# Attention scores with keys split once ahead and two heads a pass, and the order turns, scores, values on TensorE

## The chip, the core and the metric

The kernel runs on one core of one Trainium2 chip. The metric is the device time of one execution in microseconds (us), from the profiler's clock; the trace of one profiled execution shows what each engine did in it. An engine is TensorE (PE, with its weight loads shown apart as PEld), VectorE (DVE), ScalarE (ACT), GpSimd (POOL) or SyncE (SP, which here only issues DMAs).

## The reference

Two gated layers over 2048 tokens (16 blocks of 128) with 256 features: a convolution over context products, a mixture of experts with 8 routed experts (called f0), attention (called c), and a mixture with 32 routed experts (f1). The attention is where the change is:

```
x = x + tanh(g0[0]) * L0_xattn(ctx, ctx, layernorm(x), ...)     # context stage
x = x + tanh(g_ffn[0]) * L0_ffn(layernorm(x), ...)              # f0
x = x + tanh(g_xattn[1]) * L1_xattn(layernorm(x), ctx, ctx)     # attention, 16 heads of 16
x = x + tanh(g_ffn[1]) * L1_ffn(layernorm(x), ...)              # f1
# L1_xattn, with sequences of 128 tokens, so each block of 128 attends to itself:
scores = q @ k.T / 4 ; scores[k > q] = -inf ; p = softmax(scores) ; out = p @ v
```

Keys and values are both the context. The normed x and the keys are fp32, and the products of the scores are made in TensorE's reduced fp32 format (fp32r): each operand is split into a high part, rounded to it, and a low part, the rest.

## The kernel before

The four stages run one after the other, and each engine has its own written-out program; semaphores alone tie them. f0 and f1 walk over steps K: TensorE makes the hidden products of step K+1 (or K+4), then the output products of K. f0 has 64 steps of 18 or so passes of 512 columns.

The attention has 16 blocks b (128 tokens each) of 4 quads t (4 heads each), so 64 steps n = 4b + t. A step's work runs through all engines:

- scores (L1408 to L1419): into one of three PSUM banks go the causal mask (identity times a table, 512 columns, bf16), then `k_blocks_hi` and `k_blocks_lo`, each a pass of 512 columns over four heads. The stationary operand is `q_split_t`, whose 128 rows are 4 heads x 16 features for the high part and the same for the low part of the query. The moving operand is a block-diagonal array: the keys of head h stand in the rows of head h and the columns of head h, and zeros elsewhere. These blocks come from DRAM with their zeros, 256 KB a step (`load_keys`), ACT rounds them (`key_hi`, L1299) and POOL subtracts (`key_lo`, L1303), 60 times in the attention and 4 times at the end of f0.
- DVE takes each head's row maximum (`maxima`, L1598) and subtracts it into `y` (`shifted`, L1604).
- TensorE transposes `y`, four 128x128 (`turned`, L1426), ACT takes the exponential out of PSUM into `activated` (`probs`, L1567), and TensorE multiplies by the values (`values`, L1437): four products of 32 weight columns, each in its own strip of the array, which are 8 instructions in the trace since they are plain fp32.
- Once a block: the sum is copied out (`out_copy`, L1460, ACT), transposed (`out_rows`, L1446, at t = 2), and DVE divides by the sum of the probabilities, adds to X and takes moments (L1464, L1468, L1474, L1478). The queries of block b+3 are normed (L1310), rounded (L1317), subtracted (L1322, POOL); those of block b+2 are transposed (`query_turned`, L1330, four transposes at t = 3) and copied to `q_split_t` (`query_copy`, L1338).

TensorE's program in step n is: turned(n), scores(n+2), values(n), and what comes once a block. DVE's is maxima(n+1), shifted(n+1), and its once-a-block work. In steps 0 to 3 DVE also adds the last outputs of f0 to X (L241, L245); in steps 42 to 63 the first half of f1's inputs is prepared between the quads (transposes L332, router products L350, `x_lo` on DVE L342, rows L325 on ACT). In the trace, the turn of quad 0 starts at 402.73 us, that of quad 5 at 416.16, that of quad 42 at 486.95 and that of quad 63, the last, at 534.42.

```
                for n in range(NQ):
                    b, t = n // 4, n % 4
                    turned(pe, n)
                    if n + 2 < NQ:
                        scores(pe, n + 2)
                    ...
                    if n < NQ - 1:
                        values(pe, n)
```

## Time and profile before

| | |
|---|---|
| median of 3 runs | 937.21 us (936.82 to 937.28) |
| the profiled execution's own time | 935.47 us |
| its span, first to last instruction | 933.6 us |
| PE, PEld, DVE, ACT, POOL busy | 898.5, 719.5, 603.4, 551.0, 202.4 us |
| mean granted TensorE clock | 0.99 of full speed |
| attention, steps 5 to 41 | 70.79 us for 37 steps |
| attention, steps 42 to 62 | 47.47 us for 21 steps |

How to read it: a PE row's duration runs from a pass's start until its results are out, and passes are pipelined, so the distance from one start to the next says more than the duration. PE can look busy all the time while the starts stand further apart than the work needs. The PE record of L1418 begins early, at the end of its weights' request; its stream starts when that of L1414 is over.

### The profile page before, as it was taken

How to read it: one execution, taken by the hardware profiler on the slowest of the kernel's cores; microseconds unless marked ns; L12 is line 12 of the kernel's file. 1: busy time of each engine (PE TensorE's matmuls, PEld its weight loads, DVE VectorE, ACT ScalarE, POOL GpSimd, SP SyncE). 2: the span in 40 equal slices, each digit the busy share in tenths (PEclk: the TensorE clock that was granted, in tenths of full speed). 3: DMA queues.
4: the chain of work that ended last, by engine and by line, in shares of the span. 5: the costliest groups of instructions: out<-in, count | busy, mean ns of one | idle time of the engine just before them, and what ended most of it. 6: DMA issues, size and time to landing. Idle time of an engine off the chain costs nothing.

```text
span 933.6 us, 13901 instructions
## 1 busy us (share of the span) xinstructions
PE 898.5 (96%) x4704; PEld 719.5 (77%) x4704; DVE 603.4 (65%) x1390; ACT 551.0 (59%) x955; POOL 202.4 (22%) x172
## 2 busy tenths in 40 slices
PE   5899899999999999989999989999999999999998
PEld 5798788777788888856666667777788888888886
DVE  6678664465564566588888776566855466656654
ACT  3222343434444335468889677677777877777774
POOL 5899320000000012147777530000000000000000
PEclk9799999999999999999999999999999999999999
DMA  9101020333311351215554315434444244444443
GB/s 301 68 2 68 7 62 1 109 108 91 96 51 39 114 173 66 59 57 170 170 170 167 117 30 169 131 125 142 137 142 139 93 136 140 154 147 136 152 128 104
DMA packets 57957, 104.36 MB, mean 112 GB/s; under 512 B 7296, under 2 KB 13824, under 8 KB 57504
## 3 DMA queue, kind: packets, MB, share of 16 engines
q1 hardware_dynamic: 57168, 103.34, 34.5%
q8 instruction: 38, 0.62, 0.3%
q14 instruction: 31, 0.25, 0.1%
q10 hardware_dynamic: 720, 0.14, 0.1%
HBM read 101.03 MB, written 2.42 MB: 111 GB/s over the span
## 4 chain that ended last, share of the span: by engine, by line
PE 88%; DVE 5%; ACT 2%; POOL 1%; issue 1%; DMA 1%; SPq 1%; DVEq 0%; ACTq 0%; POOLq 0%
PE bank L646 37%; PE bank L682 28%; PE bank L1426 3%; PE bank L1437 2%; PE bank L1111 2%; PE bank L1113 2%; PE bank L1114 2%; PE bank L1126 2%; PE bank L1419 1%; PE bank L1418 1%; PE bank L350 1%; PE bank L1414 1%; PE bank L332 1%; DMA toeplitz<-in_kpad 1%; PE bank L1446 1%
## 5 line engine op out<-in xcount | busy, mean ns | idle before, releaser
L444 ACT ACTIVATE y_hi<-y 128x512 fp32r<-128x512 f32 x200 | 124.1, 621 | 82.2 <-DVE y L525 81.6
L539 DVE TENSOR_TENSOR y<-y,gate_rows 128x512 f32<-128x512 f32 x124 | 85.7, 691 | 120.6 <-ACT y L433 118.2
L682 PE MATMUL bank<-y_hi,w_hi 128*128 128x512 f32 x400 | 157.0, 393 | 1.5 <-DVE y_lo L308 1.0
L682 PE MATMUL bank<-y_lo,w_hi 128*128 128x512 f32 x400 | 156.5, 391 | 0.0
L682 PE MATMUL bank<-y_hi,w_lo 128*128 128x512 f32 x400 | 155.9, 390 | 0.0
L308 DVE TENSOR_TENSOR y_lo<-y,y_hi 128x512 fp32r<-128x512 f32 x196 | 134.3, 686 | 30.0 <-ACT y_hi L444 29.6
L427 ACT ACTIVATE activated<-bank 128x512 f32<-128x512 f32 x136 | 81.3, 597 | 80.9 <-PE bank L646 76.2
L646 PE MATMUL bank<-x_hi_first,w_hi 128*128 128x512 f32 x264 | 106.2, 402 | 0.7 <-DVE w_lo L303 0.7
L646 PE MATMUL bank<-x_hi_first,w_lo 128*128 128x512 f32 x264 | 104.2, 395 | 0.0
L646 PE MATMUL bank<-x_lo_first,w_hi 128*128 128x512 f32 x264 | 104.1, 394 | 0.0
L646 PE MATMUL bank<-x_hi_last,w_hi 128*128 128x512 f32 x264 | 103.9, 394 | 0.0
L646 PE MATMUL bank<-x_hi_last,w_lo 128*128 128x512 f32 x264 | 102.9, 390 | 0.0
L646 PE MATMUL bank<-x_lo_last,w_hi 128*128 128x512 f32 x264 | 102.7, 389 | 0.0
L1303 POOL TENSOR_TENSOR k_blocks_lo<-k_blocks_sb,k_blocks_hi 128x512 fp32r<-128x512 f32 x64 | 82.0, 1282 | 59.5 <-ACT k_blocks_hi L1299 59.0
L682 PEld LDWEIGHTS bank<-y_hi,w_hi 128*128 128x128 f32 x400 | 75.0, 188 | 20.4 <-DVE y_lo L308 2.9
L433 ACT ACTIVATE y<-activated 128x512 f32<-128x512 f32 x136 | 86.0, 632 | 4.3
L682 PEld LDWEIGHTS bank<-y_hi,w_lo 128*128 128x128 f32 x400 | 75.1, 188 | 16.3
L682 PEld LDWEIGHTS bank<-y_lo,w_hi 128*128 128x128 f32 x400 | 75.1, 188 | 16.2
L425 ACT ACTIVATE activated<-bank 128x512 f32<-128x512 f32 x64 | 38.3, 598 | 78.8 <-PE bank L646 78.8
L303 DVE TENSOR_TENSOR w_lo<-w_raw,w_hi 128x512 fp32r<-128x512 f32 (+1 forms) x96 | 75.1, 782 | 10.8 <-ACT w_hi L299 4.9
L299 ACT ACTIVATE w_hi<-w_raw 128x512 fp32r<-128x512 f32 (+1 forms) x100 | 69.7, 697 | 12.5 <-PE bank L682 12.5
L646 PEld LDWEIGHTS bank<-x_hi_first,w_hi 128*128 128x128 f32 x264 | 49.5, 188 | 12.5 <-DVE w_lo L303 1.0
(153 smaller groups left out, 1474.2 us busy)
## 6 DMA issues: line engine op xcount, KB each, us to landing
gate_rows<-gates SPq DMA_DIRECT2D x156, 256.0 KB, 3.7
w_raw<-in_wu SPq DMA_DIRECT2D x68, 256.0 KB, 2.6
k_blocks_sb<-in_k_blk SPq DMA_DIRECT2D x64, 256.0 KB, 4.2
w_raw<-in_wu SPq DMA_DIRECT2D x32, 384.0 KB, 3.1
v_slot<-in_v_rows SPq DMA_DIRECT2D x16, 256.0 KB, 2.6
ctx_windows<-in_ctx_win SPq DMA_DIRECT2D x3, 1024.0 KB, 11.8
toeplitz<-in_kpad SPq DMA_DIRECT2D x4, 512.0 KB, 8.7
X<-in_x SPq DMA_DIRECT2D x4, 512.0 KB, 9.2
```

Source lines behind the costliest of these rows:

```text
L299: act.activation(mem.whi[:, Nu % S, 0:WC], mem.wraw[:, Nu % S, 0:WC], ACT.Copy).then_inc(s_wh, 1)
L303: eng.tensor_tensor(mem.wlo[:, Nu % S, 0:WC], mem.wraw[:, Nu % S, 0:WC], mem.whi[:, Nu % S, 0:WC].bitcast(F32), ALU.subtract).then_inc(s_w ...
L308: eng.tensor_tensor(mem.ylo[:, K % S, :], mem.y[:, K % S, :], mem.yhi[:, K % S, :].bitcast(F32), ALU.subtract).then_inc(s_yl, 1)
L425: act.activation(mem.r[:, K % S, :], bk(2 * K % 3), ACT.Silu).then_inc(s_ac, 1)
L427: act.activation(mem.r[:, K % S, :], bk(K % 3), ACT.Relu).then_inc(s_ac, 1)
L433: act.activation(mem.y[:, K % S, :], mem.r[:, K % S, :], ACT.Square).then_inc(s_sq, 1)
L444: act.activation(mem.yhi[:, K % S, :], mem.y[:, K % S, :], ACT.Copy).then_inc(s_yh, 1)
L539: dve.tensor_tensor(mem.y[:, K % S, :], mem.y[:, K % S, :], gate, ALU.mult).then_inc(s_yd, 1)
L646: last = pe.matmul(o, w_[:, Nu % S, wc], x_[p][:, c, xs], start=(m == 0), stop=(m == 5))
L682: last = pe.matmul(acc(s)[:, c, :], w_[:, Nu % S, wc], y_[:, K % S, :], start=(n == 0 and m == 0), stop=(n == U - 1 and m == 2), skip_grou ...
L1303: pool.tensor_tensor(K2[:, n % KR, :], KM[:, n % KLR, :], K1[:, n % KR, :].bitcast(F32), ALU.subtract).then_inc(s_k2, 1)
L1426: last = pe.transpose(turn_bank(n)[:, g * P:(g + 1) * P], Ds[:, n % DR, g, :], ident[:])
```

## The change

Keys. The host no longer builds block-diagonal arrays. The keys come in as rows of 128 x 256 per block (`k_rows`). During f0, eight times, two blocks are loaded, ACT rounds them (`split_hi`), POOL subtracts (`split_lo`), and SP stores high and low parts to a DRAM tensor `k_parts` (`store_parts`, four DMAs each). The tiles that hold them are `v_slot` and `xn_split`, which the attention uses later. POOL then sets the eight `k_blocks` slots to zero once (a memset of 128 x 4096). In the attention, `load_keys` writes only the nonzero blocks, 64 partitions x 1 KB, in two DMAs a step (128 KB a step), eight slots deep; `key_hi` and `key_lo` are gone.

Scores. The 128 contraction rows are now 2 heads x (2 query parts) x (2 key parts) x 16 features, so one pass holds all four partial products of two heads and makes 256 columns. A step has two such passes (a = 0, 1), each with its own weights, in place of two passes of 512 columns over the same weights. The low-by-low product is now in.

Queries. There is twice as much of them: `query_hi` and `query_lo` write 512 columns in place of 256, with each part copied twice; `query_turned` and `query_copy` run twice a block, at t = 3 for a = 0 and at t = 0 of the next block for a = 1 (on ACT at t = 0 and t = 1). The transposes are fp32r with a rounded identity `ident_r`, in place of plain fp32.

Order. TensorE's step n is turned(n), scores(n+2), values(n-1). On ACT, `out_copy` of the block before stands behind `probs` of t = 0.

```diff
-                    if not final and K == NK - 16:
-                        attention_loads(sp)
+                    if not final:
+                        if K in (16, 18):
+                            load_raw(sp, (K - 16) // 2)
+                        if 21 <= K < 45 and K % 3 == 0:
+                            i = (K - 21) // 3
+                            store_parts(sp, i)
+                            if i + 2 < NB // 2:
+                                load_raw(sp, i + 2)
+                        if K == NK - 16:
+                            attention_loads(sp)
...
+                    for i in range(NB // 2):
+                        split_lo(pool, i)
+                    blocks_zeroed(pool)
...
+                        if 19 <= K < 43 and K % 3 == 1:
+                            split_hi(act, (K - 19) // 3)
...
-        KLR, KR, SR, DR, PR = 6, 4, 3, 3, 3
+        KR, SR, DR, PR = 8, 3, 3, 3
-        KM = sb("k_blocks_sb", [P, KLR, 4 * P])
-        K1 = sb("k_blocks_hi", [P, KR, 4 * P], F32R)
-        K2 = sb("k_blocks_lo", [P, KR, 4 * P], F32R)
+        K1 = sb("k_blocks", [P, KR, 4 * P], F32R)
-        xs = sb("xn_split", [P, 2, 4, 2, 64], F32R)
-        Q1 = sb("q_split_t", [P, 2, 4, P], F32R)
+        xs = sb("xn_split", [P, 2, 4, 2, P], F32R)
+        Q1 = sb("q_split_t", [P, 2, 2, 4, P], F32R)
...
+        def split_places(i):
+            parts = xs[:, i % 2].rearrange("p t a f -> p (t a f)")
+            return V[:, i % 2].rearrange("p h d -> p (h d)"), parts[:, 0:2 * D], parts[:, 2 * D:4 * D]
+
+        def load_raw(sp, i):
+            if i >= 2:
+                sp.wait_ge(s_k2, i - 1)
+            sp.dma_start(split_places(i)[0].rearrange("p (b f) -> p b f", b=2),
+                         k_rows[2 * i:2 * i + 2].rearrange("b p f -> p b f")).then_inc(s_kr[i % 2], 16)
+
+        def split_hi(act, i):
+            act.wait_ge(s_kr[i % 2], 16 * (i // 2 + 1))
+            if i >= 2:
+                act.wait_ge(s_ks[i % 2], 64 * (i // 2))
+            raw, high, _ = split_places(i)
+            act.activation(high, raw, ACT.Copy).then_inc(s_k1, 1)
...
+        def split_lo(pool, i):
+            pool.wait_ge(s_k1, i + 1)
+            raw, high, low = split_places(i)
+            pool.tensor_tensor(low, raw, high.bitcast(F32), ALU.subtract).then_inc(s_k2, 1)
+
+        def store_parts(sp, i):
+            sp.wait_ge(s_k1, i + 1)
+            sp.wait_ge(s_k2, i + 1)
+            for part, rows in enumerate(split_places(i)[1:]):
+                for j in range(2):
+                    place = k_parts[2 * i + j].rearrange("(g s d) f -> g s d f", s=2, d=HD1)[:, part]
+                    sp.dma_start(place, rows[:, j * D:(j + 1) * D].bitcast(F32)).then_inc(s_ks[i % 2], 16)
+
+        def blocks_zeroed(pool):
+            pool.memset(K1[:].rearrange("p n f -> p (n f)").bitcast(F32), 0.0).then_inc(s_kz, 1)
+
         def load_keys(sp, n):
-            if n >= KLR:
-                sp.wait_ge(s_k2, n - KLR + 1)
-            sp.dma_start(KM[:, n % KLR, :], k_blk[n]).then_inc(s_kl[n % KLR], 16)
+            if n >= KR:
+                sp.wait_ge(s_s, n - KR + 1)
+            for hh in range(2):
+                first = k_parts.offset + (2 * P * (n // 4) + 64 * (n % 4) + 32 * hh) * D
+                place = bass.AP(k_parts.tensor, first, [[0, 2], [D, 2 * HD1], [1, D]])
+                sp.dma_start(K1[64 * hh:64 * hh + 64, n % KR, hh * D:hh * D + D].bitcast(F32), place).then_inc(s_kl[n % KR], 16)
...
-        def key_hi(act, n):
-            act.wait_ge(s_kl[n % KLR], LOADED + 16 * (n // KLR + 1))
-            if n >= KR:
-                act.wait_ge(s_s, n - KR + 1)
-            act.activation(K1[:, n % KR, :], KM[:, n % KLR, :], ACT.Copy).then_inc(s_k1, 1)
-
-        def key_lo(pool, n):
-            pool.wait_ge(s_k1, n + 1)
-            pool.tensor_tensor(K2[:, n % KR, :], KM[:, n % KLR, :], K1[:, n % KR, :].bitcast(F32),
-                               ALU.subtract).then_inc(s_k2, 1)
...
+        def copies_of(view):
+
+            return view.rearrange("p (g f) -> p g f", f=HD1).unsqueeze(2).broadcast_to((P, NH1, 2, HD1))
+
+        def part_rows(b, part):
+            return xs[:, b % 2].rearrange("p t a (h s d f) -> p (t a h) s d f", h=2, d=2, s=2)[:, :, part]
+
         def query_hi(act, b):
             act.wait_ge(s_n, b + 1)
             if b >= 2:
-                act.wait_ge(s_xt, b - 1)
-            act.activation(xs[:, b % 2, :, 0, :], xc[:, b % 2, :].rearrange("p (q f) -> p q f", q=4),
-                           ACT.Copy).then_inc(s_hi, 1)
+                act.wait_ge(s_xt, 2 * (b - 1))
+            else:
+                act.wait_ge(s_ks[b], 64 * (NB // 4))
+            act.activation(part_rows(b, 0), copies_of(xc[:, b % 2, :]), ACT.Copy).then_inc(s_hi, 1)
 
         def query_lo(pool, b):
             pool.wait_ge(s_hi, b + 1)
-            pool.tensor_tensor(xs[:, b % 2, :, 1, :], xc[:, b % 2, :].rearrange("p (q f) -> p q f", q=4),
-                               xs[:, b % 2, :, 0, :].bitcast(F32), ALU.subtract).then_inc(s_lo, 1)
-
-        def query_turned(pe, b):
+            pool.tensor_tensor(part_rows(b, 1), copies_of(xc[:, b % 2, :]), part_rows(b, 0).bitcast(F32),
+                               ALU.subtract).then_inc(s_lo, 1)
+
+        def query_turned(pe, b, a):
+            if b + a == 0:
+                pe.wait_ge(s_ir, 1)
             pe.wait_ge(s_lo, b + 1)
-            if b > 0:
-                pe.wait_ge(s_qt, b)
+            if b + a > 0:
+                pe.wait_ge(s_qt, 2 * b + a)
             for t in range(4):
-                last = pe.transpose(x_bank[:, t * P:(t + 1) * P],
-                                    xs[:, b % 2, t].rearrange("p s f -> p (s f)").bitcast(F32), ident[:])
+                last = pe.transpose(x_bank[:, t * P:(t + 1) * P].bitcast(F32R), xs[:, b % 2, t, a, :], ident_r[:])
             last.then_inc(s_xt, 1)
 
-        def query_copy(act, b):
-            act.wait_ge(s_xt, b + 1)
+        def query_copy(act, b, a):
+            act.wait_ge(s_xt, 2 * b + a + 1)
             if b >= 2:
                 act.wait_ge(s_s, 4 * (b - 1))
-            act.activation(Q1[:, b % 2].rearrange("p t q -> p (t q)"), x_bank, ACT.Copy, scale=SCALE1).then_inc(s_qt, 1)
+            act.activation(Q1[:, b % 2, a].rearrange("p t q -> p (t q)"), x_bank, ACT.Copy, scale=SCALE1).then_inc(s_qt, 1)
...
         def attention_loads(sp):
-            for n in range(KLR):
+            for i in range(2):
+                sp.wait_ge(s_ks[i], 64 * (NB // 4))
+            sp.wait_ge(s_kz, 1)
+            for n in range(KR):
                 load_keys(sp, n)
...
-            if left in (12, 11, 4):
-                query_normed(act, {12: 0, 11: 1, 4: 2}[left])
-            if left in (11, 10, 3):
-                query_hi(act, {11: 0, 10: 1, 3: 2}[left])
-            if left in (9, 8, 7, 6):
-                key_hi(act, 9 - left)
-            if left in (6, 3):
-                query_copy(act, {6: 0, 3: 1}[left])
+            if left == 16:
+                act.activation(ident_r[:], ident[:], ACT.Copy).then_inc(s_ir, 1)
+            if left in (15, 13, 4):
+                query_normed(act, {15: 0, 13: 1, 4: 2}[left])
+            if left in (14, 12, 3):
+                query_hi(act, {14: 0, 12: 1, 3: 2}[left])
+            if left in (10, 7, 4, 1):
+                query_copy(act, (10 - left) // 6, (10 - left) // 3 % 2)
 
         def attention_ahead_pe(pe, left):
 
-            if left in (8, 5):
-                query_turned(pe, {8: 0, 5: 1}[left])
+            if left in (12, 9, 6, 3):
+                query_turned(pe, (12 - left) // 6, (12 - left) // 3 % 2)
...
-                pe.wait_ge(s_k2, n + 1)
+                pe.wait_ge(s_kl[n % KR], LOADED + 32 * (n // KR + 1))
                 if t == 0:
-                    pe.wait_ge(s_qt, b + 1)
-                pe.matmul(s_bank(n), Q1[:, b % 2, t, :], K1[:, n % KR, :], start=False, stop=False)
-                pe.matmul(s_bank(n), Q1[:, b % 2, t, :], K2[:, n % KR, :], start=False, stop=True).then_inc(s_s, 1)
+                    pe.wait_ge(s_qt, 2 * b + 2)
+                blocks = K1[:, n % KR, :].rearrange("p (h a k) -> p h a k", h=2, a=2)
+                for a in range(2):
+                    last = pe.matmul(s_bank(n)[:, a * 2 * P:(a + 1) * 2 * P], Q1[:, b % 2, a, t, :], blocks[:, :, a, :],
+                                     start=False, stop=(a == 1))
+                last.then_inc(s_s, 1)
...
-                for n in range(KLR, NQ):
+                for n in range(KR, NQ):
                     load_keys(sp, n)
...
                     turned(pe, n)
                     if n + 2 < NQ:
                         scores(pe, n + 2)
-                    if n == 0:
+                    if n == 1:
                         pe.wait_ge(f0.s_xa, 5)
-                    if n < NQ - 1:
-                        values(pe, n)
+                    if n > 0:
+                        values(pe, n - 1)
...
                     if t == 3 and b + 2 < NB:
-                        query_turned(pe, b + 2)
+                        query_turned(pe, b + 2, 0)
+                    if t == 0 and b > 0 and b + 1 < NB:
+                        query_turned(pe, b + 1, 1)
...
+                    if t < 2 and b > 0 and b + 1 < NB:
+                        query_copy(act, b + 1, t)
+                    probs(n)
                     if t == 0 and b > 0:
                         out_copy(act, b - 1)
-                    probs(n)
-                    if t == 0 and b > 0 and b + 1 < NB:
-                        query_copy(act, b + 1)
...
-                    if n + KR < NQ:
-                        key_hi(act, n + KR)
```

TensorE's program in the middle of the attention, before (L1437 values, L1426 turned, L1414 the mask, L1418 and L1419 scores, L1446 out_rows at t = 2):

```order
L1437 MATMUL bank3<-activated,v_slot 32x128 x4
L1426 MATMUL bank2<-ident,y 128x128 x4
L1414 MATMUL bank0<-causal,identb 128x512
L1418 MATMUL bank0<-k_blocks_hi,q_split_t 128x512
L1419 MATMUL bank0<-k_blocks_lo,q_split_t 128x512
L1437 MATMUL bank3<-activated,v_slot 32x128 x4
L1446 MATMUL bank3<-ident,o_t 128x128 x4
L1426 MATMUL bank2<-ident,y 128x128 x4
```

and the same place of the changed kernel (L1492 values, L1481 turned, L1466 the mask, L1472 scores, L1501 out_rows, L1382 query_turned):

```order
L1492 MATMUL bank3<-activated,v_slot 32x128 x4
L1501 MATMUL bank3<-ident,o_t 128x128 x4
L1481 MATMUL bank2<-ident,y 128x128 x4
L1466 MATMUL bank1<-causal,identb 128x512
L1472 MATMUL bank1<-k_blocks,q_split_t 128x256 x2
L1492 MATMUL bank3<-activated,v_slot 32x128 x4
L1382 MATMUL bank1<-ident_r,xn_split 128x128 x4
L1481 MATMUL bank2<-ident,y 128x128 x4
L1466 MATMUL bank0<-causal,identb 128x512
L1472 MATMUL bank0<-k_blocks,q_split_t 128x256 x2
```

The two passes of 512 columns have become two of 256. The values rows stand in the same place between scores and turns, but they are now those of the quad before.

ScalarE's program over one block before (L1460 out_copy, L1567 probs, L1338 query_copy, L1299 key_hi, L1310 query_normed, L1317 query_hi):

```order
L1460 ACTIVATE o_t<-bank 128x512
L1567 ACTIVATE activated<-bank 128x512
L1338 ACTIVATE q_split_t<-bank 128x512
L1299 ACTIVATE k_blocks_hi<-k_blocks_sb 128x512
L1567 ACTIVATE activated<-bank 128x512
L1299 ACTIVATE k_blocks_hi<-k_blocks_sb 128x512
L1567 ACTIVATE activated<-bank 128x512
L1299 ACTIVATE k_blocks_hi<-k_blocks_sb 128x512
L1310 ACTIVATE xn_c<-X,neg_mean_scaled,rstd 128x256
L1567 ACTIVATE activated<-bank 128x512
L1299 ACTIVATE k_blocks_hi<-k_blocks_sb 128x512
L1317 ACTIVATE xn_split<-xn_c 128x4x64
```

and after (L1389 query_copy, L1622 probs, L1515 out_copy, L1352 query_normed, L1368 query_hi):

```order
L1389 ACTIVATE q_split_t<-bank 128x512
L1622 ACTIVATE activated<-bank 128x512
L1515 ACTIVATE o_t<-bank 128x512
L1389 ACTIVATE q_split_t<-bank 128x512
L1622 ACTIVATE activated<-bank 128x512 x2
L1352 ACTIVATE xn_c<-X,neg_mean_scaled,rstd 128x256
L1622 ACTIVATE activated<-bank 128x512
L1368 ACTIVATE xn_split<-xn_c 128x16x32
```

The four roundings of keys a block are gone and one more copy of queries has come, ahead of the exponentials of t = 0 and t = 1.

## Rows read from the trace of the kernel before

**Rows 1.** Stretches: length, busy (x) of PE, PEld, DVE, ACT, POOL, clock, DMA, GB/s.
```profile
140.00:340.00 200.00, 199.41 (x895) 160.42 (x895) 109.68 (x208) 83.39 (x133) 2.64 (x2) 1.00 0.27 86
402.73:416.16 13.43, 10.60 (x90) 6.45 (x88) 13.09 (x33) 7.35 (x14) 6.01 (x6) 1.00 0.18 53
416.16:486.95 70.79, 70.47 (x628) 45.69 (x628) 61.95 (x123) 58.17 (x110) 54.72 (x48) 1.00 0.51 170
486.95:534.42 47.47, 45.24 (x393) 28.88 (x389) 39.42 (x69) 37.38 (x72) 31.96 (x28) 1.00 0.43 144
```

**Rows 2.** Waits in 416.16 to 486.95: us in total, times, longest.
```profile
PEld bank L1437 <- ACT activated L1567: 16.4, 37, 0.4
```

**Rows 3.** One step in order of time: start us, us, engine, line, xcount [idle before].
```profile
448.22 0.16 PEld L1437 LDWEIGHTS bank<-activated,v_slot 128*32 128x32 f32 x8 [0.44 <-ACT activated L1567]
448.25 0.69 DVE L1598 TENSOR_REDUCE max<-bank 128x4 f32<-128x512 f32 x1 [0.29 <-PE bank L1419]
448.57 0.42 PEld L1426 LDWEIGHTS bank<-ident,y 128*128 128x128 f32 x4 [0.20 <-issue]
448.96 0.10 PEld L1414 LDWEIGHTS bank<-causal,identb 128*128 128x128 bf16 x1
448.97 0.69 DVE L1604 TENSOR_TENSOR y<-bank,max 128x512 f32<-128x512 f32 x1
449.07 0.38 PE L1414 MATMUL bank<-causal,identb 128*128 128x512 bf16 x1
...
449.27 0.60 ACT L1567 ACTIVATE activated<-bank 128x512 f32<-128x512 f32 x1 [0.49 <-PE bank L1426]
449.29 0.19 PEld L1419 LDWEIGHTS bank<-k_blocks_lo,q_split_t 128*128 128x128 f32 x1
449.51 0.39 PE L1419 MATMUL bank<-k_blocks_lo,q_split_t 128*128 128x512 f32 x1
...
449.92 0.16 PEld L1437 LDWEIGHTS bank<-activated,v_slot 128*32 128x32 f32 x8 [0.44 <-ACT activated L1567]
```

**Rows 4.** Context stage, PE in order of time: passes of plain fp32.
```profile
70.09 1.57 PE L1111 MATMUL bank<-pair_products,toeplitz 128*128 128x208 f32 x8
71.50 1.04 PE L1126 MATMUL bank<-ident,weighted 128*128 128x128 f32 x8
```

**Rows 5.** End of f0 in order of time: fp32r weights loaded with nothing ahead.
```profile
372.51 0.19 PEld L646 LDWEIGHTS bank<-x_hi_last,w_hi 128*128 128x128 f32 x1
372.54 0.48 PE L646 MATMUL bank<-x_hi_last,w_hi 128*128 128x512 f32 x1
```

**Rows 6.** Weight loads at a change from whole array to 32 rows.
```profile
515.54 0.42 PEld L1446 LDWEIGHTS bank<-ident,o_t 128*128 128x128 f32 x4 [0.20 <-issue]
516.12 0.32 PEld L363 LDWEIGHTS bank<-ident,logits_t 32*128 32x128 f32 x4 [0.17 <-issue]
```

**Rows 7.** DVE in order of time, over its once-a-block work.
```profile
450.97 0.26 DVE L1464 RECIPROCAL rden<-bank 128x16 f32<-128x16 f32 x1 [0.34 <-PE bank L1446]
451.14 0.63 DVE L1604 TENSOR_TENSOR y<-bank,max 128x512 f32<-128x512 f32 x1
451.69 0.41 DVE L1468 TENSOR_TENSOR o_norm<-bank,rden 128x256 f32<-128x256 f32 x1
452.13 0.48 DVE L1474 SCALAR_TENSOR_TENSOR X<-o_norm,tg,X 128x256 f32<-128x256 f32 x1
452.54 0.68 DVE L1598 TENSOR_REDUCE max<-bank 128x4 f32<-128x512 f32 x1
453.14 0.42 DVE L1478 BATCH_NORM_STATS2 stats<-X 128x6 f32<-128x256 f32 x1
```

**Rows 8.** The same DVE line later, 508 to 511.
```profile
508.95 1.43 DVE L1474 SCALAR_TENSOR_TENSOR X<-o_norm,tg,X 128x256 f32<-128x256 f32 x1
```

**Rows 9.** POOL in the same stretch.
```profile
508.81 1.28 POOL L1303 TENSOR_TENSOR k_blocks_lo<-k_blocks_sb,k_blocks_hi 128x512 fp32r<-128x512 f32 x1 [0.37 <-ACT k_blocks_hi L1299]
```

**Rows 10.** SP's queue in order of time.
```profile
445.23 1.86 SPq L1288 DMA_DIRECT2D k_blocks_sb<-in_k_blk  x4
```

29 lines of the change are left out of this document (14 added, 15 removed).

## Prediction

> **What bounds the kernel now.** I read the stretches first [rows 1]. In f0 TensorE is busy 199.4 of 200 us; in steps 5 to 41 it is busy 70.47 of 70.79 us, DVE 61.95, ACT 58.17, POOL 54.72; steps 0 to 4 belong to DVE (13.09 of 13.43). A busy PE is not yet a fast PE, so next the waits: the weight loads of values waited for the exponential in all 37 steps, 16.4 us in total [rows 2]. Then one step by its start times [rows 3]. From the load of values at 448.22 to that of 449.92 it takes 1.70 us, in these pieces:
> - values to turned: 448.57 - 448.22 = 0.35.
> - turned to the stream of the mask: 449.07 - 448.57 = 0.50.
> - mask to the first keys pass: 449.29 - 449.07 = 0.22. The load of the second keys pass starts as the first stream does, so 449.29 marks it.
> - first to second keys pass: 449.51 - 449.29 = 0.22 to 0.23.
> - second keys pass to the load of values: 449.92 - 449.51 = 0.41. The exponential ends at 449.27 + 0.60 = 449.87, and the load starts 0.05 later.
>
> So the step is a loop: turn, exponential, values, turn, with the scores beside the exponential. Nothing that only shortens the scores would help; the new order is what opens this. Check of the whole stretch: 37 steps x 1.70 = 62.9 us; 70.79 - 62.9 = 7.9 us are 18 batches of four transposes (nine of `out_rows`, nine of `query_turned`), 0.44 each.
>
> **TensorE's step after the change.** The first two pieces and the mask stay: 0.35 + 0.50 + 0.22 = 1.07.
>
> First to second keys pass. A 256-column fp32r pass is not in the trace. The 512-column one has a pitch of 0.226, so half its columns make 0.11 to 0.12, if the next weights are in by then. What an fp32r load needs: with nothing ahead of it, it starts at 372.51 and its pass ends at 372.54 + 0.48 = 373.02 [rows 5]; a pass's record that is not held up is 0.39 [rows 3], so the stream began at 372.63, 0.11 to 0.12 after the load. The other end is the recorded load, 0.19 [rows 3]. Between them lies the plain fp32 pass of 208 columns: eight in 71.50 - 70.09 = 1.41, 0.176 each [rows 4]. I take 0.12, since load and stream both fit in it.
>
> The Trainium skill ("TensorE: Matmul & The Clock Gate", section "LDWEIGHTS (loading the stationary operand)") has a load take its column count over 1.2, which is 107 ns for 128 columns. By that the pass would be paced as I take it, and by the recorded 0.19 the sum below would lose 0.07 a step. What no row here shows: the same page in "What overlaps and what doesn't" lets a load overlap a running pass only in another row group, which would expose every load of the two shorter passes; the row of the second keys pass, whose load starts at 449.29 under a running stream, disagrees. It would give 58 x 2 x 0.11 = 12.8 more, 939, close to rival D below, and has no chance of its own.
>
> Second keys pass to values. Its stream is 0.12, and the array changes from whole to strips. The one other change of that kind is from `out_rows` to 32-row transposes [rows 6]: the next load comes 516.12 - 515.54 = 0.58 after the four transposes' first load, against 448.96 - 448.57 = 0.39 without such a change [rows 3]. The last transpose streams from about 0.39 to 0.50, so the change waits some 0.09 beyond the stream. The piece is 0.12 + 0.09 = 0.21. Upper bound: 0.41 - 0.11 = 0.30, if the wait seen today is the array's and not the exponential's (both would fit the 0.05). The exponential of quad n-1 ends 0.65 + 0.65 = 1.3 after that quad's turn, which is before turned(n), so values(n-1) waits for nobody.
>
> The step becomes 1.07 + 0.12 + 0.21 = 1.40, a gain of 0.30.
>
> **Batches.** `query_turned` runs twice a block. Today's fp32 transposes take (1.04 - 0.27)/7 = 0.11 each [rows 4]; an fp32r transpose is not in the trace. Half a 256-column pass would be 0.06, the recorded load 0.19. I keep 0.11, that is 0.44 a batch, the nearest row. A block is then 4 x 1.40 + 3 x 0.44 = 6.92 against 4 x 1.70 + 2 x 0.44 = 7.68.
>
> **Does DVE keep up?** Its work is unchanged. From max to shift 0.72 [rows 3], from shift to the next operation about 0.60, so a plain step needs 1.32. At t = 3 [rows 7]: max 0.60, reciprocal 0.17, then 0.55, 0.44, 0.41, together 2.17. At t = 0: 0.60, moments 0.42 by their duration, 0.60, together 1.62. A block needs 2 x 1.32 + 2.17 + 1.62 = 6.43, under 6.92. In latency: scores(n+2) are ready about 0.50 + 0.22 + 0.12 + 0.28 + 0.04 = 1.16 after turned(n) starts, max and shift end 1.41 later, so turned(n+2) could start at 2.6; two steps take at least 2.8, and those with batches 3.2. The reserve is thin but positive.
>
> **The other engines.** An ACT operation on 128 x 512 takes 0.6 [rows 3]; ACT loses four of them a block, the roundings, and gains one copy and half of one in `query_hi`, so about 1.5 us a block less. Its copies ahead of the exponential at t = 0 and 1 push it by at most 0.6, and its reader is now a step later. POOL loses 1.28 a step [rows 9]. SP issues eight key DMAs and one of values a block; four take 1.86 [rows 10], so 8 x 0.47 + 0.33 = 4.1 of 6.9 us. The loads run eight steps ahead, 8 x 1.7 = 14 us; today's six are 6 x 1.9 = 11. In f0: eight roundings on ACT and eight subtractions on POOL (idle there) of 0.6 and 1.3 us, in an f0 step of 18 passes x 0.23 = 4.1. SP stands in `store_parts` until they are done, with `gate_rows` and weights queued behind; it runs four steps ahead of their users and loses about two and a half. The memset and 16 first key loads (7.5 us of issue) come in a stage where the same four steps of 4.1 cover them.
>
> What could uncover f0: DVE's x update took 1.43 when a POOL subtraction had started 0.14 before it, and 0.48 otherwise [rows 7 to 9]. By the Trainium skill ("SBUF — State Buffer", section "SBUF: two separate sides"), a VectorE operation with two SBUF inputs and a GpSimd operation that reads SBUF lock each other out; the rows agree. It speaks against the eight subtractions in f0 and for the 60 that go. DVE is idle 45% of f0 [rows 1], 1.9 us of each 4.1, more than one subtraction of 1.28. I cost it at nothing; with the cover gone it is at most 8 x 1.28 = 10.2 us.
>
> **Sum**, against the profiled execution's own 935.5:
> - steps 0 to 4: nothing, DVE paces them.
> - steps 5 to 41: 37 x 0.30 = -11.1; nine more batches, +4.0: -7.1.
> - steps 42 to 62: 21 x 0.30 = -6.3; four more batches, +1.8; TensorE stood still there for 47.47 - 45.24 = 2.2 us [rows 1], while ACT and POOL were full of keys; of that I count -1.4. Against it the preparation of f1 goes through DVE's `x_lo` between quads, which a shorter step uncovers: +1.5. Together -4.4.
> - f0: two more batches of query transposes, +0.9.
>
> The sum is -10.6, so 924.9; the median stands 1.7 above the profiled time, so **926.6**.
>
> **Rivals.**
> - A, as above, TensorE paces at 1.40 to 1.45: 923 to 929. Chance 0.48.
> - B, the change to strips costs what it seems to today: second pass to values 0.30. 58 steps x 0.09 = +5.2: 932. For it: no step shows values without the exponential just done. Against: rows 6. Chance 0.15.
> - C, the fp32r transpose goes at 0.06: 4 x 0.05 in each of 30 query batches (18 in steps 5 to 41, 8 after, 4 in f0) = -6.0; a block is then 6.5, next to DVE's 6.43: 920.6. Chance 0.15.
> - D, the other side: the recorded 0.19 of an fp32r load sets the pace of every short pass. 58 steps x 0.07 = +4.1, 30 query batches x 4 x 0.08 = +9.6: 940, slower. For it: the change makes 128 short passes and 128 short transposes, and the one short non-transposing pass goes at 0.176, not at its recorded load's 0.19 but not below either. Against: the load in rows 5. The gain of 10.6 is used up at 10.6/(58 + 120) = 0.06 above 0.11, so from 0.17 on. Chance 0.10.
> - E, gains are given back in waits: DVE late after its t = 3 work, f1's preparation, or the eight subtractions in f0; half the gain: 930 to 935. Chance 0.12.
>
> **Range and chances.** The range leaves out D and the far end of C: 919.5 to 936. The rest holds somewhat over 8 in 10. Faster by over 0.2% (which is about what a measurement of this kernel can tell from no change, 1.9 us) are A, B, C, most of E and nothing of D: 0.87. Within 0.2%: 0.04. Slower: 0.09.
>
> **What the changed profile would show.** Start to start of the two 256-column passes 0.12 (D: 0.19); from the second to the load of values 0.21 (B: 0.30), with no wait for the exponential in that row; turned to turned 1.40 in plain steps and 6.9 a block; query transposes 0.11 apart (C: 0.06); DVE's max waiting for the scores in most steps, and turned hardly ever for DVE; f0 the same but for 0.9. I would be wrong if turned waits for DVE in every block, if the key loads show up as a releaser of the scores, or if y_lo releases output passes in f0 where it did not before.

## The result and the profile after

The changed kernel takes 1011.5 us (median of 4 runs, 1010.3 to 1011.8) against 937.0 (4 runs, 936.2 to 937.3): ratio 1.079, interval 1.078 to 1.081. It is slower by 74.5 us; forecast were 926.6 and at most 936.

First the stretches of the kernel after: the end of f0, steps 0 to 4, and the rest of attention in two parts; the columns are those of [rows 1].

```profile
300.00:400.00 100.00, 89.31 (x399) 73.32 (x399) 51.53 (x87) 37.00 (x61) 10.17 (x6) 0.95 0.27 89
417.63:430.59 12.96, 9.11 (x86) 6.63 (x84) 12.62 (x33) 5.21 (x10) 2.64 (x2) 1.00 0.00 0
430.59:486.95 56.36, 38.10 (x344) 24.62 (x345) 32.42 (x59) 22.77 (x43) 6.88 (x7) 0.97 0.21 66
486.95:609.30 122.35, 84.82 (x727) 53.90 (x725) 68.72 (x133) 52.75 (x99) 13.20 (x11) 0.94 0.22 69
```

Attention begins at 417.63 in place of 402.73 [rows 1], 14.9 later. From its quad 0 to its quad 63 it takes 609.26 - 417.63 = 191.6 us, and 131.7 before: 59.9 more. Together that is the whole loss. No engine is full behind step 5 (TensorE 38 of 56 us, with 66 GB/s where [rows 1] have 170), so something is waited for. (The granted clock is 0.97 and 0.94 there, where TensorE stands idle so often; what that adds by itself was not measured.) The waits of the kernel after in 430 to 600 name the second part (us in total, times, longest):

```profile
PEld bank L1472 <- DMA k_blocks<-k_parts: 75.2, 52, 1.9
PE bank L1472 <- DMA k_blocks<-k_parts: 54.0, 49, 1.5
DVE max L1651 <- PE bank L1472: 64.8, 49, 2.2
```

The scores wait for their keys in nearly every step, a wait that the kernel before does not have. In its place stands no wait of values for the exponential [rows 2]. Next SP's queue of the kernel after, in order of time, where the first 16 key loads are issued in f0, and one pair in attention:

```profile
320.78 0.37 SPq L385 DMA_DIRECT2D gate_rows<-gates  x1
321.26 19.34 SPq L1341 DMA_DIRECT2D k_blocks<-k_parts  x16
340.64 1.81 SPq L1397 DMA_DIRECT2D causal<-in_causal_c  x1
342.49 0.43 SPq L1398 DMA_DIRECT2D identb<-in_identb_c  x1
342.97 0.91 SPq L1346 DMA_DIRECT2D v_slot<-in_v_rows  x2
343.98 0.37 SPq L385 DMA_DIRECT2D gate_rows<-gates  x1
...
446.43 3.26 SPq L1341 DMA_DIRECT2D k_blocks<-k_parts  x2
```

Sixteen loads hold SP for 19.34 us, 1.2 each; forecast were 7.5 in all. `gate_rows` stands behind them and leaves 23.2 us after the one before it, more than the 16.4 (four steps of 4.1) that the prediction had as cover. What follows, first VectorE and TensorE of the kernel after, each in order of time, then its stretches with the clock:

```profile
351.47 0.69 DVE L534 TENSOR_TENSOR y<-activated,gate_rows 128x512 f32<-128x512 f32 x1 [13.73 <-issue]
...
343.25 0.39 PE L660 MATMUL bank<-x_hi_last,w_lo 128*128 128x512 f32 x1
354.33 0.79 PE L696 MATMUL bank<-y_hi,w_hi 128*128 128x512 f32 x1 [10.69 <-DVE y_lo L309]
```

```profile
345.00:350.00 5.00, 0.00 (x0) 0.00 (x0) 0.00 (x0) 0.00 (x0) 0.00 (x0) 0.77 0.96 298
350.00:355.00 5.00, 0.67 (x2) 0.58 (x3) 2.52 (x4) 2.08 (x4) 0.00 (x0) 0.50 0.62 217
355.00:360.00 5.00, 5.00 (x17) 3.94 (x16) 2.71 (x5) 2.00 (x4) 1.35 (x1) 0.70 0.38 134
```

TensorE stands still for 10.69 us, and works on at the lower of its clock's two levels (0.50 is 1.2 GHz) until about 358. The standstill and the slower passes behind it (about 3.7 us at half the clock, so 1.8) make 12.5 of the first part's 14.9. The trace names no releaser for VectorE's 13.73; that it stood for the late gate rows is read from SP's order, and experiment 1 bears it out.

What TensorE does when it has its keys is as forecast. A plain step of the kernel after, before the ring of keys runs dry:

```profile
430.59 0.42 PEld L1481 LDWEIGHTS bank<-ident,y 128*128 128x128 f32 x4 [0.36 <-DVE y L1657]
430.98 0.10 PEld L1466 LDWEIGHTS bank<-causal,identb 128*128 128x128 bf16 x1
431.09 0.41 PEld L1472 LDWEIGHTS bank<-k_blocks,q_split_t 128*128 128x128 f32 x2
431.63 0.16 PEld L1492 LDWEIGHTS bank<-activated,v_slot 128*32 128x32 f32 x8
431.99 0.31 PEld L1481 LDWEIGHTS bank<-ident,y 128*128 128x128 f32 x3 [0.20 <-DVE y L1657]
```

From turn to turn 431.99 - 430.59 = 1.40, and the load of values has no wait in front.

So why is a key load slow? Each moves 64 partitions from 32 rows of DRAM taken twice. Counting the trace's DMA records between 460 and 475 us gives the time in which so many rows of one size were under way at once (rows of 1 KB of the kernel after; of 2 KB in experiments 3 and 12):

```
kernel        row    median ns   most of the 15 us
after         1 KB   48          2 rows: 12.1 us
experiment 3  2 KB   87          2 rows: 13.2 us
experiment 12 2 KB   87          4 rows: 11.3 us
```

The theory, S: the two-fold outermost dimension of the source leaves a load only two DMA engines. By an estimate from these rows it takes 32 x 0.048 = 1.5 us on both, two loads 3.0 us a step, and a load of values comes on top once a block. From the turn of quad 12 (449.24) to that of quad 52 (574.36) a step took 3.13. (191.6/64 = 2.99, used in experiment 8's expectation, averages in the first steps, whose keys were already in the eight slots.) The queue fills, and from then on an issue takes 1.38 in the median, about as long as a load needs. By the Trainium skill ("DMA: Bandwidth & Descriptors", section "Why a DMA increments its semaphore by 16 and not by 1", under "How many engines (k)") a transfer gets the largest number up to 16 that divides the slowest dimension of both its access patterns; here 2 and 64, so two, and the counts agree. Rivals: a source read twice is slow by itself, or each load costs SP 1.38 whatever engines serve it.

### The profile page after: what moved, and what is told of

Same layout as the page of the kernel before. It is cut to its first block, busy times and chain, and to the rows that moved or that the text cites. A ratio compares the mean times of both kernels' runs of the same rounds, so it can differ in the third digit from the quotient of the medians.

```text
span 1008.5 us, 14027 instructions
## 1 busy us (share of the span) xinstructions
PE 908.4 (90%) x4768; PEld 726.5 (72%) x4768; DVE 605.0 (60%) x1390; ACT 532.3 (53%) x916; POOL 143.3 (14%) x117
## 4 chain that ended last, share of the span: by engine, by line
PE 72%; DMA 13%; SPq 5%; DVE 4%; issue 3%; ACT 1%; POOL 1%; DVEq 0%; ACTq 0%; POOLq 0%
PE bank L660 34%; PE bank L696 26%; DMA k_blocks<-k_parts 12%; SPq L1341 4%; PE bank L1125 2%; PE bank L1127 2%; PE bank L1128 2%; PE bank L1140 2%; PE bank L351 1%; DMA toeplitz<-in_kpad 1%; PE bank L1472 1%; PE bank L333 1%; PE bank L233 1%; DMA gate_rows<-gates 0%; DVE stats L1182 0%
## 5 line engine op out<-in xcount | busy, mean ns | idle before, releaser
L696 PEld LDWEIGHTS bank<-y_hi,w_lo 128*128 128x128 f32 x400 | 75.4, 188 | 16.4
L1651 DVE TENSOR_REDUCE max<-bank 128x4 f32<-128x512 f32 x64 | 44.2, 690 | 69.5 <-PE bank L1472 69.4
L1472 PE MATMUL bank<-k_blocks,q_split_t 128*128 128x256 f32 x128 | 34.4, 353 | 55.8 <-DMA k_blocks<-k_parts 55.7
```

Source lines behind the costliest of these rows:

```text
L696: last = pe.matmul(acc(s)[:, c, :], w_[:, Nu % S, wc], y_[:, K % S, :], start=(n == 0 and m == 0), stop=(n == U - 1 and m == 2), skip_grou ...
L1472: last = pe.matmul(s_bank(n)[:, a * 2 * P:(a + 1) * 2 * P], Q1[:, b % 2, a, t, :], blocks[:, :, a, :], start=False, stop=(a == 1))
L1651: dve.tensor_reduce(nmax[:, n % DR, :], s_bank(n).rearrange("p (h k) -> p h k", k=P), AX_X, ALU.max).then_inc(s_m, 1)
```

## The experiments

Experiments 1 to 4, 5 to 8, 9 to 12 and 13 each shared a chip, on which the kernel before took 936.57, 936.85, 936.28 and 936.85. They are told by question: first the loads (1, 2, 3, 12, 7, 8), then f0 (6), then the order (4, 5, 9, 10, 13), and one last edit (11).

**1. The repeated rows stored twice, so that a load reads 64 plain rows.** Against the changed kernel (the stores' semaphore counts double with it):

```
-        k_parts = nc.dram_tensor("k_parts", (NB, 2 * P, D), ...
+        k_parts = nc.dram_tensor("k_parts", (NB, 4 * P, D), ...
+                    for c in range(2):      # around each store
-                place = bass.AP(k_parts.tensor, first, [[0, 2], [D, 2 * HD1], [1, D]])
+                place = bass.AP(k_parts.tensor, first, [[D, 4 * HD1], [1, D]])
```

> The changed kernel, but k_parts holds each group of 32 key rows twice (eight stores for each pair of blocks in place of four), so that a key load reads 64 plain rows in place of 2 x 32 rows with the outer step zero. Bytes, destinations and number of loads stay the same. Theory S (the outermost dimension of the source, 2, puts a load on two DMA engines, 32 rows of 1 KB each, 32 x 0.048 = 1.5 us): the issue of a load falls from 1.38 to about 0.48 us, no score waits for keys, the stop of TensorE near 338 us goes, steps take 1.4 us plain and a block 6.8; total 922 to 932. Rival R (64-partition loads of 1 KB rows, or two a step, cost the queue their 1.4 us whatever the source's shape; or reading a DRAM tensor written by this kernel does): total stays at 1005 to 1015.

934.1 us (932.4 to 935.5), ratio 0.997, interval 0.996 to 0.998. Attention took 116.9 in place of 191.6, and the scores waited for keys 0.6 us in all, so S holds there. The stop near 343 us is gone too: the same 16 loads from plain rows held SP for 10.11 us, and TensorE was busy 100.00 of the 100 us from 300 to 400. The total missed the expected range (922 to 932) because f0 was late again, by 12.9. SP's queue of this kernel shows another cause than in the changed one, and one of its waits in 130 to 415 the effect:

```profile
213.69 5.02 SPq L1331 DMA_DIRECT2D k_parts<-xn_split  x8
218.75 0.74 SPq L1309 DMA_DIRECT2D v_slot<-in_k_rows  x1
219.53 0.86 SPq L294 DMA_DIRECT2D w_raw<-in_wu  x1
220.50 0.84 SPq L385 DMA_DIRECT2D gate_rows<-gates  x2
```

```profile
DVE y L534 <- DMA gate_rows<-gates: 13.8, 3, 6.4
```

SP waits for a split, issues eight stores, and only then the gate rows.

**2. The changed kernel without its key loads after the first eight steps**, so that later steps use old keys:

```
                 for n in range(KR, NQ):
-                    load_keys(sp, n)
-            pe.wait_ge(s_kl[n % KR], LOADED + 32 * (n // KR + 1))
+            pe.wait_ge(s_kl[n % KR], LOADED + 32)
```

> The changed kernel, but only the first eight steps' keys are loaded (16 loads near the end of f0) and the slots are used again, so the scores after step 7 are of other keys. It leaves out 112 of 128 key loads. Theory S and rival R both: no wait for keys after step 7, so the attention shows what TensorE and DVE need: plain step 1.40, block 6.8 to 6.9. The 16 slow loads stay, so the stop of 14 us near 338 us stays: total 935 to 945. If the attention's steps stay well above 1.5 us, something other than the loads is slow there.

935.7 us (934.1 to 938.9), ratio 0.999, interval 0.998 to 1.000. Attention took 116.5, the same steps as in 1. So the loads cost attention 75 us, and doubled rows cost it nothing; f0's stop of 10 us stayed (TensorE busy 89.84 of the 100 us from 300), as did the first 16 loads.

**3. The kernel before, its key loads from a two-fold source** (rows 64 to 127 of a step's keys equal rows 0 to 63, so the data are the same):

```
-            sp.dma_start(KM[:, n % KLR, :], k_blk[n])
+            place = bass.AP(k_blk.tensor, k_blk.offset + n * P * 4 * P,
+                            [[0, 2], [4 * P, P // 2], [1, 4 * P]])
+            sp.dma_start(KM[:, n % KLR, :], place)
```

> The kernel before, but each key load reads the first 64 of its 128 source rows twice, through a source with outermost dimension 2 and step zero (so the keys are partly others). Bytes (256 KB), destination (128 partitions x 2 KB) and number of loads are those of before. Theory S: each load runs on two engines, 64 rows of 2 KB each at 0.084 = 5.4 us, against a step of 1.9: the attention goes to about 5.4 us a step, total 1130 to 1180. Rival R: the destination and row size are those of before, so nothing changes: 935 to 942.

1157.0 us (one run). The form of the source alone, without anything else of the change, costs 220 us; a step took 5.6 us, near the 5.4 of two engines.

**12. The same with `[[0, 4], [4 * P, P // 4], [1, 4 * P]]`**; it reads the first 32 rows of keys four times and leaves out the others.

> The kernel before (936.9 us), in which the load of each step's keys reads the first 32 rows four times, from a source whose outermost dimension is four-fold, in place of 128 different rows; the bytes and the row length are the same, the keys are not those of the reference. Theory E (a load runs on as many DMA engines as its source's outermost dimension has entries): four engines, 128 rows x 0.087 / 4 = 2.8 us a load, and a step cannot go faster: attention 64 x 2.8 = 178 in place of 131.7, total 975 to 990, with four rows of 2 KB under way at a time. Rival R (any repeated source runs on two engines): about 1157 as with the two-fold one. Rival N (four engines are enough, hidden behind the steps): 936 to 945.

997.6 us (one run): above the range, but four rows were under way as the table above shows. Attention took 184 (178 expected) and began 9 us later, which I had left out. So the rows under way follow the outermost number, and reading a row four times costs less than reading it twice. The stores of experiment 1 agree where nothing is repeated: the outermost dimension of their destination is 8 (the groups of keys), and in the 8 us from 213.69, when eight of them run, 8 rows of 1 KB were under way for 2.4 us, longer than any other number. A two-fold source whose two parts differ was not tried.

**7. Each key load as two of 32 plain rows**, on the changed kernel, four a step (the scores wait for twice the count):

```
-                place = bass.AP(k_parts.tensor, first, [[0, 2], [D, 2 * HD1], [1, D]])
+                place = bass.AP(k_parts.tensor, first, [[D, 2 * HD1], [1, D]])
+                for c in (64 * hh, 64 * hh + 32):    # around the load
```

> The changed kernel (1011.5 us) with its own k_parts, in which each key load of 64 partitions from a repeated source of 2 x 32 rows is written as two loads of 32 partitions from 32 plain rows: four issues a step in place of two, the same bytes and the same rows of 1 KB. Theory E (what costs is that a load with the two-fold outermost dimension runs on two DMA engines; 32 plain rows spread over 16): an issue is 0.4 to 0.6 us, four a step 1.6 to 2.4 us, so that steps go at 1.8 to 2.4 us where the plain step needs 1.39 and 1.78, attention 118 to 150, total with the first stage's loss of 15 to 20 us 937 to 975. Rival I (SP's issue of 1.38 us is a price of each load as such, whatever engines it runs on): four a step 5.5 us, total above 1150.

945.3 us (944.2 to 946.8), ratio 1.009, interval 1.008 to 1.011. Rival I falls, and so does a price of reading twice: these loads, too, read every row twice. SP's queue of this kernel shows the bound that is left:

```profile
439.73 7.39 SPq L1342 DMA_DIRECT2D k_blocks<-k_parts  x16
447.16 0.42 SPq L1347 DMA_DIRECT2D v_slot<-in_v_rows  x1
447.62 8.77 SPq L1342 DMA_DIRECT2D k_blocks<-k_parts  x16
456.44 0.42 SPq L1347 DMA_DIRECT2D v_slot<-in_v_rows  x1
```

SP never rests: 17 issues are 7.8 to 9.2 us a block (0.46 each at the least), more than the 6.7 that TensorE needs by experiment 6, and attention took 135.5. It began 7.0 us later than before, which is the rest.

**8. The second load of each step issued by ACT behind its exponential**, on the changed kernel (`load_keys` takes `halves`; SP issues half 0, ACT half 1 from step 8 on).

> The changed kernel (1011.5 us) with the loads as they are, but from step 8 on the second load of each step is issued by ACT behind the step's exponential in place of SP. Theory E (the load runs on two DMA engines, 32 rows of 1 KB by 0.048 us each = 1.5 us on each of both, two loads a step = 3.0 us, which is the pitch of 191.6/64 = 2.99 measured): if both queues' loads fall on the same two engines nothing is gained, 1005 to 1020. Rival Q (SP's issue of 1.38 us is what bounds a step, 2 x 1.38 + the load of values; halved on each queue): pitch 1.8 to 2.0 us, attention 118 to 130, total 945 to 955. In between (970 to 995) would say that the second queue's loads fall on other engines in part, or that ACT's issues cost the exponential.

1005.9 us (one run). ACT's issues took 0.49 each, SP's mostly 0.48, and still a step took 3.13 from quad 12 to quad 52, the pace of the changed kernel, with two rows of 1 KB under way for 12.0 of 15 us. A second queue brings no further engines; rival Q falls.

**6. Doubled rows, and SP's program of f0 spread**, on experiment 1:

```
-                        if 21 <= K < 45 and K % 3 == 0:
-                            i = (K - 21) // 3
+                        if 24 <= K < 48 and K % 3 == 0:
+                            i = (K - 24) // 3
                             store_parts(sp, i)
...
+                        if NK - 16 <= K < NK - 8:
+                            load_keys(sp, K - NK + 16)
-                        if K == NK - 16:
+                        if K == NK - 8:
                             attention_loads(sp)      # now without the key loads
```

> The kernel with doubled stored rows (934.1 us), with three things later in SP's program of the first stage and nothing else: the stores of a split pair stand at K = 24+3i in place of 21+3i, the raw load behind them too, and the first 16 key loads are spread two a step from K = 48 to 55, the other loads of attention at K = 56. Theory (the first stage's loss of 12.9 us is SP standing before a store that waits for its split, so that gate rows and weights come late): no wait of VectorE for gate rows, TensorE's idle time between 130 and 300 back to under 1 us, no clock below 1.0 there, attention begins at 403 to 406, total 921 to 926. Rival (the loss is the added work on ACT and POOL, or the DMA queue itself filled with stores): attention begins above 411, total 930 to 936.

923.4 us (922.2 to 925.3), ratio 0.986, interval 0.984 to 0.988. Its stretches, to be set against [rows 1]:

```profile
130.00:300.00 170.00, 169.41 (x755) 134.94 (x754) 94.08 (x203) 76.63 (x123) 10.76 (x8) 1.00 0.39 122
300.00:400.00 100.00, 100.00 (x458) 82.54 (x457) 58.13 (x96) 42.39 (x70) 11.46 (x7) 1.00 0.33 100
...
417.94:482.21 64.27, 62.38 (x650) 47.88 (x664) 61.01 (x123) 45.14 (x84) 14.08 (x13) 1.00 0.43 119
482.21:522.80 40.59, 39.90 (x403) 30.01 (x405) 37.28 (x69) 30.45 (x57) 6.10 (x5) 1.00 0.39 113
```

f0's stops are gone, and attention begins at 405.25. Up to 300 us the stores and the raw loads are what has moved; which of the two counts was not separated.

**4. The new order alone, on the kernel before:**

```
-                    if n < NQ - 1:
-                        values(pe, n)
+                    if n > 0:
+                        values(pe, n - 1)
```

with ACT's `out_copy(b - 1)` behind the exponential in place of ahead of it.

> The kernel before with the new order alone (turned n, scores n+2, values n-1, and out_copy behind probs). By the prediction's pieces the wait for the exponential, 0.09 us a step, goes: 58 steps x 0.09 = -5 us, 932. Rival: the time from the second keys pass to the values, 0.41, is the array's change to strips, and nothing is gained: 937. A third: DVE's chain (two steps 2.6 us against 3.2) sets a new limit and the time rises.

946.7 us (945.9 to 947.8), ratio 1.011, interval 1.009 to 1.012: slower, where I had expected 932. Plain steps took 1.61, 0.09 less than before, as the prediction's pieces have it; but steps with t = 2 took 2.93 and those with t = 3 2.3 to 3.1. It isn't DVE's chain, the third theory: the turns waited for DVE 6.6 us in all in 405 to 545, and 4.5 before. The waits of this kernel in 405 to 545:

```profile
PEld bank L1418 <- POOL k_blocks_lo L1303: 20.7, 28, 1.5
...
ACT k_blocks_hi L1299 <- DMA k_blocks_sb<-in_k_blk: 20.0, 20, 1.8
```

**5. The old order, on experiment 1** (both edits of 4 undone).

> The kernel with doubled stored rows (934.1 us), and TensorE's order of the kernel before: turns of quad n, scores of n+2, values of n itself. Keys are split once and need no ACT or POOL work in a step, as in the changed kernel. Theory (the two parts need each other; the order is worth something only when the scores no longer wait for a split made in the step): plain step 1.39 + 0.1 to 0.3 because TensorE again waits for the exponential (0.58 us) between turns and values, minus nothing else, so attention 117 + 64 x 0.15 to 0.3 = 127 to 136, total 944 to 953. Rival (the gain lies in the split alone, the order is worth nothing): attention 117 to 119, total 933 to 936.

955.9 us (954.8 to 956.5), ratio 1.020, interval 1.018 to 1.022, above the expected range. Each against the kernel before on its chip, that is +19.1 where experiment 1 has -2.5: the order is worth 21.5 there. Plain steps are 1.73 again, and the wait for the exponential is back (25.7 us, 46 times, 1.0 at most, in 422 to 520, where [rows 2] have 0.4 at most): ACT copies queries twice a block ahead of it. Not all of it is TensorE's order: steps with t = 1, 2 and 3 are 0.31 to 0.34 longer than in experiment 1, those with t = 0 0.80 (2.55 against 1.75), where ACT copies both queries and output ahead of the exponential. The old order with these copies behind it was not tried. Keys split once, without the order, make attention 139.5, slower than before; neither part as written gains anything alone.

**9. Experiment 4 with POOL's subtraction cut from 512 to 16 columns** from step 4 on; the rest of the low part is left out.

```
+            w = 4 * P if n < KR else 16
-            pool.tensor_tensor(K2[:, n % KR, :], ...
+            pool.tensor_tensor(K2[:, n % KR, 0:w], ...
```

> The kernel before with the new order (946.7 us), and POOL's subtraction that makes the low part of the keys cut from 512 columns to 16 from step 4 on, so that the low part of the keys is left out but for those columns; all waits stay. Theory V (the order alone loses because the values of a quad now end a step later, the load of values in SP's queue waits for them, and the key loads behind it come late: ACT's copy of the high part waits for DMA): ACT's waits for the key load stay at 8 us in 430 to 475, only the 1.28 us of POOL behind each late copy go, attention 142.5 to about 128, total 930 to 935. Theory P (POOL's 1.28 us a step is itself the pace, the waits for DMA are its echo): ACT's waits for the load go, the block is 4 x 1.61 + turns 0.88 = 7.3, attention 122 to 126, total 925 to 930.

932.9 us (931.6 to 935.1); attention 128.6, and ACT's waits for the load in 430 to 475 stayed (8.6 us in place of 8.1). As V has it; and since the total is 3.4 below the kernel before, where 4 is 10.1 above, those waits cost what they do only with POOL's 1.28 us behind them.

**10. Experiment 4 with SP's values load behind the keys of step 4b+3:**

```
-                    if n % 4 == 0 and n // 4 >= 2:
+                    if n % 4 == 3 and n // 4 >= 2:
                         load_values(sp, n // 4)
```

> The kernel before with the new order (946.7 us), and SP's load of the values of a block three places later in its program, behind the keys of step 4b+3 in place of 4b; nothing else. Theory V (the key loads queued behind the values load, which waits for values that now end a step later, are what is late): ACT's wait for the key load in 430 to 475 falls from 8.1 us to under 1, the steps t = 2 and 3 from 2.93 and 2.3 to about 2.0, block 7.3 to 7.5, attention 124 to 128, total 928 to 933. Theory P (POOL's subtraction sets the pace): nothing changes, 943 to 948.

942.4 us (942.3 to 942.7), between the two ranges and nearer P's. ACT's wait for the load fell to none and t = 3 to 2.07, so V names a wait that was there, but it was only 4.0 of the 10.1 us by which the order had lost (+6.1 in place of +10.1); t = 2 stayed at 2.93. ACT and POOL of this kernel show what was left:

```profile
441.45 0.60 ACT L1460 ACTIVATE o_t<-bank 128x512 f32<-128x512 f32 x1 [0.47 <-PE bank L1437]
441.95 0.59 ACT L1338 ACTIVATE q_split_t<-bank 128x512 fp32r<-128x512 f32 x1
442.42 0.63 ACT L1299 ACTIVATE k_blocks_hi<-k_blocks_sb 128x512 fp32r<-128x512 f32 x1
...
443.13 2.52 POOL L1303 TENSOR_TENSOR k_blocks_lo<-k_blocks_sb,k_blocks_hi 128x512 fp32r<-128x512 f32 x2 [1.65 <-ACT k_blocks_hi L1299]
```

The copy of the output waits for values that now end a step later; the split of keys stands behind it, and POOL idles 1.65.

**13. Experiment 10 with ACT's `key_hi` ahead of `out_copy` in steps t = 0.**

> The kernel with the new order and the values load behind the keys of step 4b+3 (942.4 us), and ACT's copy of the high part of the keys of step n+4 put ahead of the copy of the output and of the queries in steps t = 0, in place of behind them; nothing else. Theory A (the copy of the output waits in ACT's queue for values that now end a step later, and the copy of the keys behind it makes POOL start at 443.13 in place of 441.48, so that the scores of step t = 2 wait 1.05): POOL no longer idles there, the step t = 2 takes 2.0 to 2.1 in place of 2.93, over 13 blocks -11, total 930 to 934. Theory P (POOL's 1.28 us a step has no room in a block of 7.5, whatever the order): the wait moves to t = 3 or 0, the block stays above 8, 939 to 943.

931.0 us (930.8 to 931.7), ratio 0.994, interval 0.992 to 0.996. Step t = 2 took 2.01. The order with both edits gains 5.8 us on the kernel before, near the 5 that 58 x 0.09 promised. What the two edits would do in the old order was not tried, so that all of it is the order's is likely by the plain step (1.61 against 1.70) and not shown.

**11. Experiment 6 with VectorE's variances a step earlier** (`n == 4 * 10 - 3`).

> The kernel with doubled rows and later stores (923.4 us), with VectorE's variances of the last stage's first half behind step 37 in place of 38. Theory (step 40 takes 3.31 in place of 1.76 because these variances, 0.9 us, push the update of x by 0.5 us, so that it starts together with POOL's subtraction and takes 1.575 in place of 0.485): the update takes 0.485, step 40 takes 1.8, total 921.5 to 922.5. Rival (VectorE has no room at step 37 either and the turns of 38 or 39 wait as long): 923 to 924.

922.5 us (922.4 to 922.7), ratio 0.985, interval 0.984 to 0.987. VectorE's update of that step, first in experiment 6, beside POOL's subtraction, then here:

```profile
477.66 1.57 DVE L1534 SCALAR_TENSOR_TENSOR X<-o_norm,tg,X 128x256 f32<-128x256 f32 x1
...
476.73 0.48 DVE L1534 SCALAR_TENSOR_TENSOR X<-o_norm,tg,X 128x256 f32<-128x256 f32 x1
```

Step 40 fell from 3.31 to 1.97, but step 38 rose from 1.78 to 2.07. This is the best version, but against the kernel before on its chip it gains 13.8 where experiment 6 gains 13.4, which the runs don't tell apart.

## Why the prediction was wrong, by its own steps

**The step that failed** is the one on SP: "SP issues eight key DMAs and one of values a block; four take 1.86 [rows 10], so 8 x 0.47 + 0.33 = 4.1 of 6.9 us". The 0.47 is that of a load of 128 plain rows, and the changed loads took it only while the queue was not full, the first four of a row. Issued often is not the trouble: experiment 6 issues eight plain loads a block, and its scores wait for keys 1.7 us in all. The changed loads need 1.5 us each on two engines, by the estimate above, and SP was held to 1.38 in the median. The same price stands in "the memset and 16 first key loads (7.5 us of issue)": they took 19.34, and 10.69 us of TensorE's standstill followed; even from plain rows they took 10.11. I costed a DMA by how many are issued and not by the shape of its source, and listed the key loads as a releaser only among the signs of being wrong. None of the five rivals has this wait. The pace of two loads on two engines (3.0 us a step by estimate, 3.13 measured) accounts for attention's 59.9, and experiment 2 takes it away by taking the loads away.

**Where these loads are plain and f0's queue is spread**, the forecast can be read off experiment 6, span against span (922.8 and 933.6). The -10.8 is close to the sum's -10.6, but that is in part luck: the parts below miss by up to 2.5 and cancel. One batch of query transposes there:

```profile
477.17 0.39 PEld L1387 LDWEIGHTS bank<-ident_r,xn_split 128*128 128x128 f32 x4 [0.20 <-issue]
```

Part by part:
- Plain step: 1.40 forecast, 1.39 to 1.40 measured, no wait for the exponential. Right, and D, B fall: in experiment 6 the two 256-column passes start at 478.22 and 478.34 and the load of values at 478.55, so 0.12 and 0.21, as forecast.
- Batches: 0.44 forecast, 0.38 measured; the four query transposes start 0.084 apart (their loads at 477.17, 477.25, 477.34, 477.42 in experiment 6), between A's 0.11 and C's 0.06. A block took 1.39 + 1.78 + 1.78 + 1.76 = 6.71, not 6.92.
- DVE: the turns waited for it 4.7 us in all, 1.5 at most.
- Steps 5 to 41: 64.27 against 70.79, -6.5 (forecast -7.1). 1.5 of it is the one step 40, in which the 1.57 of [rows 8]'s kind appeared.
- Steps 42 to 62: 40.59 against 47.47, -6.9 (forecast -4.4). TensorE's idle time there fell from 2.2 to 0.7, as forecast; the +1.5 for f1's preparation did not show.
- Steps 0 to 4: 12.69 against 13.43, -0.7 (forecast 0).
- Start of attention: 405.25 against 402.73, +2.5 (forecast +0.9). Behind attention +0.8.

**"it runs four steps ahead of their users and loses about two and a half"** held for the four stores a pair that it was said of: TensorE was busy 169.4 of 170 us from 130 to 300, as before. But there was no room for eight (experiment 1: 162.9). Experiment 6 has the stores three steps later and lost nothing.

**"The new order is what opens this"** is not true of the order alone. On the kernel before it cost 10.1 us as it is, and the total came out 5.8 below the kernel before only with the edits of 10 and 13; on experiment 1 it was worth 21.5, ACT's order included. I never asked what was queued behind the operations that wait for values. With the new order, taking the keys out from behind them gave back 4.0 (SP) and 11.9 (ACT), by experiments 10 and 13.

What stays open: whether the +2.5 ahead of attention is the four query batches alone; what the edits of 10 and 13 give in the old order; and how a load with rows outermost and a two-fold middle dimension would do. The last two were not tried.

## What to carry to other kernels

Cost a DMA by its shape before its count: read the outermost dimension of both sides, and if it is small, count rows x time per row / engines against the step it feeds; then ask what stands behind it in the issuing queue. When an operation moves a step later, look at every queue for what waits on it and what is queued behind that: here a load of values and a copy of the output turned the order's gain into a loss. A change of two parts is to be costed with either part alone as well.

## What the runs showed of the hardware

- A load from a two-fold source keeps two rows under way (issued by SP alone or by SP and ACT together), from a four-fold one four (SP). Rows took 48 ns (1 KB) and 87 ns (2 KB) in them.
- An issue on SP took 0.48 to 0.56 us for the first four two-engine loads in a row, and 1.38 in the median behind them; 0.42 for loads of 32 plain rows; 0.57 to 0.7 for stores of 128 KB.
- fp32r transposes of 128 x 128 run 0.084 apart, against 0.11 in plain fp32 [rows 4].
- VectorE's update of 128 x 256 took 1.575 when it started within 0.01 us of POOL's subtraction, and 0.485 when 0.47 ahead of it (experiment 6).
